# GLU gate and up products as two float32r passes over a split activation; last layer's quantisers on integers, the norm's in bf16 with reordered channels

## The reference

```python
# layer 2
W = (wq - 128.0) * scale[:, None]              # integers 0..31, 704 hidden channels
out = qlinear(silu(qlinear(x, gate)) * qlinear(x, up), down)
# layer 3
h = bf16((x - mean) * rsqrt(var + 1e-5) * w + b)
def mx_quant(x):                               # blocks of 32 along the contraction
    scale = 2 ** (floor(log2(max|x| of the block)) - 6)
    return clip(round(x / scale), -128, 127) * scale
h = bf16(mx_quant(h) @ mx_quant(W1).T + b1)
h = bf16(gelu_tanh(h))
h = bf16(mx_quant(h) @ mx_quant(W2).T + b2)
out = bf16(bf16(x) + h)
```

## Time and profile before

| | |
|---|---|
| time, median of 3 runs | 479.6 us (479.38 to 480.41) |
| profiled execution | 479.51 us, span 477.6 us |
| PE busy | 397.5 us, 83% of the span |
| weight loads busy | 346.4 us, 73% |
| VectorE busy | 347.0 us, 73% |
| ScalarE busy | 292.2 us, 61% |
| GpSimd busy | 77.0 us, 16% |
| mean granted TensorE clock | 0.914 |

### The profile page before, as it was taken

How to read it: one execution, slowest core, us unless ns; L and a number is a source line. 1 busy time by engine, 2 the same in 40 slices (tenths; PEclk the granted TensorE clock), 3 DMA queues, 4 the chain that set the end, 5 groups by cost and what they waited for, 6 DMA issues and landing times.

```text
span 477.6 us, 7259 instructions
## 1 busy us (share of the span) xinstructions
PE 397.5 (83%) x2576; PEld 346.4 (73%) x2576; DVE 347.0 (73%) x521; ACT 292.2 (61%) x513; POOL 77.0 (16%) x96
## 2 busy tenths in 40 slices
PE   3999672997852689999999999999869997999463
PEld 3998640776732689999999999999747876787332
DVE  5999979695658999999999049500223568989885
ACT  5996764689870576676676675674422456575462
POOL 3000102000110321221121110380175000000000
PEclk9999887898985599999999999999958999999857
DMA  7500000000178218411603865500032000000000
GB/s 280 185 1 1 2 0 0 1 0 1 55 256 304 50 29 283 143 32 36 220 30 109 304 230 162 197 21 23 22 93 85 0 1 0 12 13 12 12 11 33
DMA packets 23668, 38.80 MB, mean 81 GB/s; under 512 B 2233, under 2 KB 18250, under 8 KB 23506
## 3 DMA queue, kind: packets, MB, share of 16 engines
q1 hardware_dynamic: 15442, 23.39, 14.6%
q10 hardware_dynamic: 5920, 8.65, 5.3%
q0 software_dynamic: 2272, 6.30, 4.4%
HBM read 33.10 MB, written 5.24 MB: 80 GB/s over the span
## 4 chain that ended last, share of the span: by engine, by line
PE 56%; DVE 20%; issue 12%; ACT 9%; another core or an unknown queue 1%; DMA 1%; POOL 1%; ACTq 0%; POOLq 0%; SPq 0%; DVEq 0%
PE bank L1454 18%; PE bank L1435 17%; PE bank L1503 5%; PE bank L1299 3%; PE bank L1512 2%; PE bank L1270 2%; DVE scr L773 2%; DVE scr L775 2%; PE bank L1427 1%; DMA v<-in_kT 1%; PE bank L1317 1%; POOL small L349 1%; DVE small L1179 1%; DVE w3T L791 1%
## 5 line engine op out<-in xcount | busy, mean ns | idle before, releaser
L1435 PE MATMUL bank<-big,yT 128*128 x384 | 86.7, 379 | 0.0
L589 ACT ACTIVATE yT<-bank,big 128x128 f32<-128x128 f32 x192 | 54.5, 369 | 50.3 <-PE bank L1454 47.4
L1435 PEld LDWEIGHTS bank<-big,yT 128*128 128x128 f32 x384 | 71.2, 190 | 8.7
L365 POOL DMA_INDIRECT xg<-token_rows,rowi x24 | 31.8, 1326 | 143.1 <-PE bank L1427 119.9
L1503 PE MATMUL bank<-yT,scr 128*128 128x256 f32 x192 | 44.8, 390 | 3.8 <-DVE yT L1118 2.8
L1503 PEld LDWEIGHTS bank<-yT,scr 128*128 128x128 f32 x192 | 36.9, 196 | 9.6 <-issue 3.2
L349 POOL TENSOR_TENSOR small<-small 128x2 f32<-128x2 f32 (+1 forms) x9 | 10.1, 1120 | 185.6 <-DVE small L1145 80.2
L1270 PE MATMUL bank<-identf,scr 128*128 128x128 f32 x240 | 31.9, 294 | 3.8 <-DVE scr L786 3.8
L1454 PE MATMUL bank<-ygT,w3T 128*128 128x128 f32 x256 | 31.8, 285 | 3.1 <-ACT ygT L581 3.1
L1454 PEld LDWEIGHTS bank<-ygT,w3T 128*128 128x128 f32 x256 | 31.5, 202 | 3.8 <-issue 3.4
L1270 PEld LDWEIGHTS bank<-identf,scr 128*128 128x128 f32 x240 | 31.0, 211 | 4.1 <-DVE scr L786 4.0
(11 more groups left out here) (332 smaller groups left out, 826.2 us busy)
## 6 DMA issues: line engine op xcount, KB each, us to landing
big<-in_moe_w SPq DMA_DIRECT2D x16, 1024.0 KB
slot_outputs<-yo ACTq DMA_DIRECT2D x24, 128.0 KB
v<-in_kT SPq DMA_DIRECT2D x2, 512.0 KB, 4.8
big<-in_gateT SPq DMA_DIRECT2D x1, 1024.0 KB, 7.3
big<-in_upT SPq DMA_DIRECT2D x1, 1024.0 KB, 9.4
big<-in_downT SPq DMA_DIRECT2D x1, 1024.0 KB, 11.7
x<-in_x_bsc SPq DMA_DIRECT2D x1, 1024.0 KB, 14.1
token_rows<-y POOLq DMA_DIRECT2D x4, 256.0 KB, 7.4
```

The lines of the kernel that those rows point to most:

```text
L365: gp.indirect_dma_start(out=xg[:, j % 3], out_offset=None, in_=Y1, in_offset=bass.IndirectOffsetOnAxis(ap=rowi[:, j:j + 1], axis=0)).then_ ...
L589: ins = sc.activation(hT[j % 2][:, c], ps[1 + 2 * (j % 2) + c // 4][:, (c % 4) * P:(c % 4 + 1) * P], ACT.Gelu, bias=b1s[:, c, j:j + 1])
L1435: ins = te.matmul(ps[5 + 2 * (j % 2)][:, 0:C], hT[j % 2][:, c], big[:, bass.ds(at + (W2_AT + c * C), C)], start=(c == 0), stop=(c == IC - 1))
```

## The change

It does five things.

2. ScalarE's list: the second weight copy of the experts moves behind `copy_xT(0)`, the Gelu table in front of it; the Sigmoid table is loaded after the last expert tile's gelu, the Silu table after `head_y2(0)`.
3. `gelu_quant`: rounding and the upper clip become one tensor_scalar that writes int16; the last multiply reads int16.
4. `norm_scales` and `norm_quant`: scale and inverse as bf16 bit patterns, multiply, clip to int16, multiply.
5. The channels of the normalised activation and of layer 3's first weight matrix are stored in the order (position in block, block), so that the eight block scales repeat along the row.

```diff
+        with nc.sbuf_tensor("y2r", [P, 2, 2, KC, 256], F32R) as y2r:
+            pass
         v = sb("v", [P, KC, NT])
+        with nc.sbuf_tensor("qgu", [P, 2, KC, HQ], F32R) as qgu:
+            pass
...
-            copy_w1(1)
-            sc.preload_act_table(ACT.Gelu)
-
             def copy_xT(j):
...
+            sc.preload_act_table(ACT.Gelu)
             act.wait_ge(s["b1s_ready"], 1)
             copy_xT(0)
+            copy_w1(1)
...
                 gelu_tile(j)
+                if j == TILES - 1:
+                    sc.preload_act_table(ACT.Sigmoid)
...
+            def head_y2(p):
+                act.wait_ge(s["y2_ready"], p + 1)
+                if p >= 2:
+                    act.wait_ge(s["gu2_ready"], HC2 * (p - 1))
+                sc.activation(y2r[:, p % 2, 0], yT[:, :, 256 * p:256 * (p + 1)], ACT.Copy).then_inc(s["y2h_ready"], 1)
...
             sigmoid_l2(0)
+            head_y2(0)
+            sc.preload_act_table(ACT.Silu)
             for p in range(G + 2):
...
+                if p >= 1 and p + 1 < G:
+                    head_y2(p + 1)
                 if p < G:
                     for c in range(2, HC2):
                         silu_l2(p, c)
                 if p == 0:
                     sigmoid_l2(1)
+                    head_y2(1)
...
-                ve.tensor_tensor(w3q[:, m].rearrange("p (n j) -> p n j", j=32), w3v, half, ALU.subtract).then_inc(s["w3q"], 1)
+                if m == 0:
+                    ins = ve.tensor_tensor(w3q[:, 0].rearrange("p (r j n) -> p r n j", r=HC3, n=NB), w3v.rearrange("p (r n) j -> p r n j", n=NB),
+                                           half.rearrange("p (r n) j -> p r n j", n=NB), ALU.subtract)
...
             dve.wait_ge(s["ld_l2"], 48)
-            ve.tensor_scalar(qgu, qgu.bitcast(I32), 128.0, None, ALU.subtract)
+            dve.wait_ge(s["w3q"], 2)
+            ve.tensor_scalar(qgu[:], qgu_i, 128.0, None, ALU.subtract)
...
+            def rest_y2(p):
+                dve.wait_ge(s["y2h_ready"], p + 1)
+                c = slice(256 * p, 256 * (p + 1))
+                if p >= 2:
+                    dve.wait_ge(s["gu2_ready"], HC2 * (p - 1))
+                ve.tensor_tensor(y2r[:, p % 2, 1], yT[:, :, c], y2r[:, p % 2, 0].bitcast(F32), ALU.subtract).then_inc(s["y2T_ready"], 1)
...
+                bits = top3.bitcast(I32).rearrange("p (t n) -> p t n", t=2).unsqueeze(2).to_broadcast([P, 2, 4, NB])
+                ve.tensor_scalar(hinverse.bitcast(I16).rearrange("p (t q n) -> p t q n", t=2, q=4), bits, -1.0 / 65536, 260.0 * 128, ALU.mult, ALU.add)
+                link(ve.tensor_scalar(hunit.bitcast(I16).rearrange("p (t q n) -> p t q n", t=2, q=4), bits, 1.0 / 65536, -6.0 * 128, ALU.mult, ALU.add))
...
+                link(ve.tensor_tensor(by_block(hb), by_block(hb), of_scale(hinverse), ALU.mult))
+                link(ve.tensor_scalar(hb.bitcast(I16), hb, 127.0, None, ALU.min))
                 if p >= 2:
                     dve.wait_ge(s["hq3_tr"], p - 1)
...
+                ve.tensor_tensor(by_block(hq[p % 2]), by_block(hb.bitcast(I16)), of_scale(hunit), ALU.mult).then_inc(s["hq3"], 1)
...
-                link(ve.tensor_scalar(t, t, MAGIC, MAGIC, ALU.add, ALU.subtract))
-                link(ve.tensor_scalar(t, t, 127.0, None, ALU.min))
+                link(ve.tensor_scalar(t.bitcast(I16), t, 127.0, None, ALU.min))
...
-                ve.tensor_tensor(q3[i % 2].rearrange("p (r i) -> p r i", r=HC3), t3,
+                ve.tensor_tensor(q3[i % 2].rearrange("p (r i) -> p r i", r=HC3), t3.bitcast(I16),
                                  unit.unsqueeze(1).to_broadcast([P, HC3, P]), ALU.mult).then_inc(s["q3_ready"], 1)
...
                 if p < G:
                     gate_l2(p, 2)
+                if p >= 1 and p + 1 < G:
+                    rest_y2(p + 1)
                 if 1 <= p <= G:
                     norm_quant(p - 1)
...
                 if p == 0:
-                    scale_y2T(1)
+                    scale_y2(1)
+                    rest_y2(1)
...
-                if c == 0:
-                    pe.wait_ge(s["y2T_ready"], p + 1)
...
+                for part in range(2):
+                    if c == 0:
+                        pe.wait_ge(s["y2T_ready" if part else "y2h_ready"], p + 1)
+                    for m in range(2):
+                        for k in range(KC):
+                            ins = te.matmul(bank_of((p, c))[:, m * 256:(m + 1) * 256], qgu[:, m, k, c * P:(c + 1) * P],
+                                            y2r[:, p % 2, part, k], start=(part == 0 and m == 0 and k == 0),
+                                            stop=(part == 1 and m == 1 and k == KC - 1))
```

More of the change, by code:

```diff
@@ L9 @@
 F32 = mybir.dt.float32
+F32R = mybir.dt.float32r
 BF16 = mybir.dt.bfloat16
@@ L101, in bass_adaln_ffn_stack @@
         yr = [y1[:], g[:, 0].rearrange("p k (a c) -> p (k a) c", c=C)]
-        qgu = scr[:, 0:3072].rearrange("p (m k h) -> p m k h", m=2, k=KC)
+        qgu_i = scr[:, 0:3072].bitcast(I32).rearrange("p (m k h) -> p m k h", m=2, k=KC)
         qd = scr[:, 3072:4608].rearrange("p (c n) -> p c n", c=HC2)
@@ L1152, in norm_apply @@
                 for t in range(2):
-                    ins = ve.scalar_tensor_tensor(hb[:, t], xh[:, t], r_[:, 2 * p + t:2 * p + t + 1], lnb, ALU.mult, ALU.add)
+                    ins = ve.scalar_tensor_tensor(hb[:, t].rearrange("p (j n) -> p n j", n=NB), xh[:, t].rearrange("p (n j) -> p n j", n=NB),
+                                                  r_[:, 2 * p + t:2 * p + t + 1], lnb.rearrange("p (n j) -> p n j", n=NB),
+                                                  ALU.mult, ALU.add)
@@ L1154, in norm_apply @@
                 link(ins)
+            hunit = xh[:, 0, 0:64].bitcast(BF16)[:, 0:64]
+            hinverse = xh[:, 0, 0:64].bitcast(BF16)[:, 64:128]
             def norm_scales(p):
-                hb3 = hb.rearrange("p t (n j) -> p (t n) j", j=32)
-                link(ve.tensor_reduce(ex3[:, 0, 0:16], hb3, AX.X, ALU.max, apply_absolute_value=True))
-                link(block_scales(16))
-            def norm_quant(p):
-                hb3 = hb.rearrange("p t (n j) -> p (t n) j", j=32)
-                xh3 = xh.rearrange("p t (n j) -> p (t n) j", j=32)
-                link(ve.tensor_tensor(hb3, hb3, ex3[:, 2, 0:16].unsqueeze(2).to_broadcast([P, 16, 32]), ALU.min))
-                link(ve.tensor_tensor(xh3, hb3, ex3[:, 1, 0:16].unsqueeze(2).to_broadcast([P, 16, 32]), ALU.add))
+                top3 = ex3[:, 0, 0:16]
+                link(ve.tensor_reduce(top3.rearrange("p (t n) -> p t n", t=2), hb.rearrange("p t (j n) -> p t n j", n=NB),
+                                      AX.X, ALU.max, apply_absolute_value=True))
+                link(ve.tensor_scalar(top3.bitcast(I32), top3.bitcast(I32), 0x7F800000, None, ALU.bitwise_and))
+                link(ve.tensor_scalar(top3, top3, 2.0 ** -120, None, ALU.max))
+                bits = top3.bitcast(I32).rearrange("p (t n) -> p t n", t=2).unsqueeze(2).to_broadcast([P, 2, 4, NB])
+                ve.tensor_scalar(hinverse.bitcast(I16).rearrange("p (t q n) -> p t q n", t=2, q=4), bits, -1.0 / 65536, 260.0 * 128, ALU.mult, ALU.add)
+                link(ve.tensor_scalar(hunit.bitcast(I16).rearrange("p (t q n) -> p t q n", t=2, q=4), bits, 1.0 / 65536, -6.0 * 128, ALU.mult, ALU.add))
@@ L1206, in _ @@
             combine(0)
-            scale_y2T(0)
+            scale_y2(0)
+            rest_y2(0)
             for p in range(G + 2):
@@ L1215, in _ @@
                 if p >= 1 and p + 1 < G:
-                    scale_y2T(p + 1)
+                    scale_y2(p + 1)
                 if p < G:
@@ L1500, in gate_up_l2 @@
                     pe.wait_ge(s[of], count)
-                for m in range(2):
-                    for k in range(KC):
-                        ins = te.matmul(bank_of((p, c))[:, m * 256:(m + 1) * 256], qgu[:, m, k, c * P:(c + 1) * P],
-                                        yT[:, k, 256 * p:256 * (p + 1)], start=(k == 0), stop=(k == KC - 1))
+                for part in range(2):
[6 more added lines that the diff above has]
+                                            stop=(part == 1 and m == 1 and k == KC - 1))
                 ins.then_inc(s["gu2_ready"], 1)
```

17 lines of the change are left out of this document (11 added, 6 removed).

## The result

The changed kernel takes 483.94 us (482.28 to 485.06) where the kernel before, timed beside it, takes 479.69 (479.38 to 481.23): ratio 1.0082, interval 1.0067 to 1.0097. It is slower by 4.25 us, and 16.4 above the forecast. The profiled execution took 484.05 us, with a span of 482.3.

A forecast was written before the change was run, and what follows sets the result against it. PE bounds the experts; in the last layers PE and VectorE are both near full, finally VectorE alone. Start -2.5, entry -0.65, stage 0 -5.5, the rest -4.1, clock +0.8: 479.5 becomes 467.5 us, range 464 to 471 (473.5 including rival (b)).

The forecast's parts named there:

- The unknown stall: Stage 0, between two silus: ScalarE loses 4.56 us to something unknown, PE about 1; if it stays, 4.5 gained.
- stage 0: Third layer, PE's first product to first residual add: 19.95 us becomes 14.4 through cheaper products, -5.5.
- The norm part: VectorE's norm quantiser in the last layers: three operations of 0.69 become 1.13 us in all, -0.94 per call.
- The strided reads and writes of the reordered channels: VectorE's operations on reordered channels: already at one element a cycle, so 0 to +0.2 us each.
- rival (c): The four stages: PE, less busy, drops to its lower clock; 37 us more, 504 us; chance of being decisive 0.06.
- The products: Gate and up products as float32r: 112 ns each, a chunk 0.90 instead of 1.73 us, 20 us off PE.
- Rival (a): Products: float32r costs as much as float32 or is bound by weight loading; 5 us gained, 474.5 us; chance 0.13.
- Start of the experts: ScalarE's reordered copies and Gelu table let PE's first expert product start earlier: -2.5 us, clock worth 1.3 either way.
- Entry: Entry to the third layer: Sigmoid table load moved away, -1.28, head copy added, 0.60 plus 0.05; net -0.65 us.
- rival (b): VectorE's new operations miss fast modes: q3's multiply 1.22 for 0.69, norm_quant 0.3 to 0.5 more; 473 us; chance 0.13.
- Stages 1 to 3: Residual add to residual add in the last layers: VectorE's savings less added rest give -0.7, -0.5 and -1.0 us.
- The end: After the last residual add, VectorE's: -0.94 for the norm and two of three gelu_quants, -1.9 us.

The follow-up runs named there:

- e9: The changed kernel, unaltered, timed once more: 483.81 us, ratio 1.0069 to the kernel before.
- e13: The changed kernel, unaltered, timed a third time in another session: 476.60 us, ratio 0.9935 to the kernel before.
- e14: e5 unaltered, timed again beside e13: 477.25 us, ratio 0.9944 to the kernel before.
- e17: e16 unaltered, timed again in another session as control of e18: 476.06 us, ratio 0.9919 to the kernel before.
- e18: e17 with the gathers of tiles 4 to 7 held until stage 0's gates are done: 472.65 us, ratio 0.9836.
- e15: e1 unaltered, timed again beside e13: 470.93 us, ratio 0.9801 to the kernel before.
- e5: The changed kernel with a GpSimd memset between the gathers of tiles 1 and 2, shifting later gathers: 477.35 us, ratio 0.9958.
- e7: The changed kernel with added bf16 matmuls of no use where PE would wait: 473.27 us, ratio 0.9865.
- e2: The changed kernel, reordered channels kept, but norm_apply reads strided and writes contiguously: 471.79 us, ratio 0.9819.
- e1: The changed kernel with the norm's quantiser and the channel order of layer 3's first weights put back as before: 471.01 us, ratio 0.9805.
- e6: The changed kernel with the norm in natural order up to the scaling, which reads strided and writes contiguously: 473.13 us, ratio 0.9851.
- e16: The changed kernel with e6's norm and e7's added matmuls on PE: 469.27 us, ratio 0.9767 to the kernel before.

## Why the prediction was wrong

The forecast was 467.5; measured were 483.94 us. The miss of 16.4 us has two causes, of 6 to 7 and of 10 us; without both the forecast is met within 0.4, which is partly luck, since its other terms missed by up to 1.2 us both ways.

**The unknown stall: 6.1 us by stage 0, 6.6 to 7.3 by the medians (e9's and the first comparison's against e13's and e14's, whose starts are earlier too). The step that failed: "PE loses about 1 of it. If it stays, I get 4.5."** The profile before had shown it, and I priced it as a share of a fixed delay. It is no delay but a date: the releases of chunks 2 to 4 come through just after the last gather is in, about 367 us, and the gathers hang on the experts' end and did not get shorter. With float32 products PE had its own work until 358.28 + 10.42 = 368.70, so the date cost it only the 0.97 us that the prediction read there. With the cheap products it was idle from 363.29. A stage of 15.4 became one of 21.5. The stall was hidden behind PE's work, and the speed-up uncovered it. e17 against e18 shows that the gathers in flight are what holds the releases back; e13 beside e9 shows that it happens in some sessions only. What a session has that another lacks stays open.

**The norm part: 10 us, two terms.** The quantiser itself was right (three operations for 1.13 us; 1.14 measured). The step that failed: "The strided reads and writes of the reordered channels go with operations that already run at one element a cycle (0 to +0.2 each)." The write cost +0.97 an operation (two in a pair) and the reduction +0.38. Instead of -0.94 a pair it is +1.39 of arithmetic, and in times: e13 and e14, 476.6 and 477.25, against e15's 470.93, 5.7 to 6.3 us where 3.8 were to be gained. By stages e14 is over e15 by 2.55, 1.11, 1.15 and, at the end, 1.94. About 1.45 us of stage 1 is rival (c) on a small scale, the lower clock (e5 against e7); that the norm's reordering causes it is not shown, since e2's stage 1 has it without the slow write.

**What held.** Without the norm part the forecast was 467.5 + 3.8 = 471.3; e1 and e15 took 471.01 and 470.93. By steps (e1 over before): stage 0 -4.55 against -5.5 for that case. The products go at 120 ns each at the full clock where I took 112, inside the bounds of 110 to 130. e1's stage 0 shows where the missing 1 us went (the lower clock held for three chunks and not two, so PE's 48 products took 8.33 us where 7.7 were forecast, and the add came 0.53 after the down product, behind VectorE's `combine`):

```profile
355.75 8.33 PE L1532 MATMUL bank<-y2r,qgu 128*128 128x256 f32 x48 [2.23 <-ACT y2r L661]
...
365.17 5.45 PE L1542 MATMUL bank<-scr,big 128*128 128x256 f32 x24 [0.65 <-DVE big L1150]
...
371.15 0.68 DVE L1156 TENSOR_TENSOR x<-x,bank 128x512 f32<-128x512 f32 x1
```

Rival (a) is refuted. Start of the experts -1.3 to -1.55 (changed, e1) where I took -2.5: the first product is 2.03 earlier, but the clock did not rise earlier with it, as the 1.3 us of doubt had it; where it did rise earlier (e13) the start is 4.3 earlier. Entry -1.0 against -0.65. Int16 inputs stay at 0.69 us for 1024 columns: rival (b) is refuted. Stages 1 to 3 of e1 sum to 0.23 above before; forecast without the norm were +0.6, and 0.8 more for the clock: 1.2 off, which with the end makes good what the start and stage 0 lacked. The end gave -1.87, forecast -0.96 without the norm. The range and the 0.06 for slower were wrong because two terms were given bounds from operations of another access pattern and from a wait whose end was not looked up. Rival (c) in its full form did not occur: the granted clock was 0.79 to 0.93 by stage, not 0.5. Yet from the first add to the last it was 0.88, so the sign that I had set for (c), below 0.9 there, came without (c)'s 504 us: it was a poor sign. PE's transposes were held 0.68 us by combine(2), under the 1 us that the last sign named.

## What to carry to other kernels

A wait that the profile calls unknown has an end that can be found: look what finishes just before it, and ask whether the faster engine now runs into that date. An access pattern is part of an operation's price: a row of the same shape but contiguous bounds nothing for a strided write. Here the reordering was cheap where it was read strided and written contiguously (+0.23 an operation in e2 against +0.97); at which step it is done mattered little (VectorE saves 0.10 a pair in e2, 0.18 in e6). The same program moved by 1.5% between sessions while the kernel before moved by 0.2%: repeat a small difference in another session beside a control.

e16 (natural order up to the scaling, PE kept busy) is the fastest version, 469.27 us without the stall and 476.35 and 476.06 with it; e18's held-back gathers give 472.65 in a session with the stall.
